# Folding two adapted linear layers on one core: the first product by pairs of k over all columns, the bias sum dealt out in single steps, the folded adapters stored in three chunks, and sixteen turns of the identity as TensorE's first work

## The reference

```python
x = x + L0_ffn(L0_cond(x, lang_ids))
x = x + L1_ffn(L1_cond(x, slot_ids))
```

```python
# L0_cond: x @ W.T + 2 * top-2 gated LoRA (8 experts of rank 16, a bias of 5.0 for the batch's language)
# L0_ffn : top-1 gated LoRA alone, no base product
# L1_cond: x @ W.T + b + 2 * (x @ lora_As[slot]) @ lora_Bs[slot]   (one adapter per batch, 32 slots)
# L1_ffn : y @ W_base.T + b_base + 2 * top-2 gated LoRA
```

## Time and profile before

| | |
|---|---|
| time, median of 3 runs | 466.93 us (466.07 to 467.23) |
| the profiled execution: its own time | 465.49 us |
| its span, first to last instruction | 463.6 us |
| PE busy | 446.5 us (96%) |
| DVE, ACT, POOL busy | 307.6, 154.8, 68.6 us |
| moved by DMA | 37.08 MB |

### The profile page before, as it was taken

One profiled execution on the slowest core, in us unless ns is written; L12 is line 12 of the kernel. 1 busy time (PEld: TensorE's weight loads), 2 busy tenths in 40 slices (PEclk: granted clock), 3 DMA queues, 4 the chain that ended last, 5 costly groups with the idle time before them and its releaser, 6 DMA issues.

```text
span 463.6 us, 7831 instructions
## 1 busy us (share of the span) xinstructions
PE 446.5 (96%) x2758; PEld 414.8 (89%) x2758; DVE 307.6 (66%) x916; ACT 154.8 (33%) x325; POOL 68.6 (15%) x61
## 2 busy tenths in 40 slices
PE   4999989999969999999999999999999999999997
PEld 4988989999968898889899999999999999999986
DVE  4856675656996788578467648738747755864852
ACT  5754363202122463234233224224323423321310
POOL 1100000000002411402402222120140230220110
PEclk9999999999998999999999999999999999999999
DMA  8973651101110101104102201211210310300202
GB/s 270 386 216 134 207 216 45 47 0 47 53 39 6 50 23 49 47 17 145 47 11 104 79 17 62 98 46 62 98 45 17 139 54 1 111 7 1 107 2 90
DMA packets 16287, 37.08 MB, mean 80 GB/s; under 512 B 2551, under 2 KB 7929, under 8 KB 16254
## 3 DMA queue, kind: packets, MB, share of 16 engines
q1 hardware_dynamic: 16158, 36.66, 23.1%
q0 software_dynamic: 96, 0.00, 0.0%
HBM read 27.07 MB, written 9.59 MB: 79 GB/s over the span
## 4 chain that ended last, share of the span: by engine, by line
PE 72%; DVE 14%; SPq 6%; DMA 3%; issue 2%; ACT 2%; DVEq 0%; ACTq 0%
PE banks L1334 22%; PE banks L1336 22%; PE banks L1335 22%; SPq L330 5%; DVE b_acc L1097 3%; DVE G L852 3%; PE banks L1422 2%; PE banks L1567 2%; DMA ws_lo_raw<-in_W_dram 2%; DMA b0lo_raw<-in_W_dram 1%; DVE ws_lo L852 1%; PE banks L1349 1%; SPq L362 1%; DVE x_raw L998 1%; DVE left L852 1%
## 5 line engine op out<-in xcount | busy, mean ns | idle before, releaser
L1334 PE MATMUL banks<-G,left 128*128 128x460 f32 x224 | 88.0, 393 | 0.0
L1335 PE MATMUL banks<-G,left 128*128 128x460 f32 x224 | 82.9, 370 | 0.0
L1336 PE MATMUL banks<-G,left 128*128 128x460 f32 x224 | 82.9, 370 | 0.0
L1334 PE MATMUL banks<-WbThi,ws_hi 128*128 128x460 f32 (+1 forms) x192 | 68.4, 356 | 9.8 <-DVE WbTlo L852 5.5
L509 POOL TENSOR_TENSOR xTlo<-x_raw,xThi 128x512 fp32r<-128x512 f32 x28 | 37.9, 1373 | 209.7 <-DVE hg L910 107.4
L1336 PE MATMUL banks<-WbThi,ws_lo 128*128 128x460 f32 (+1 forms) x192 | 67.0, 349 | 0.0
L1335 PE MATMUL banks<-WbTlo,ws_hi 128*128 128x460 f32 (+1 forms) x192 | 66.9, 348 | 0.0
L561 ACT ACTIVATE left<-x_raw 128x512 fp32r<-128x512 f32 x64 | 38.7, 627 | 59.9 <-DVE x_raw L998 29.3
L1334 PEld LDWEIGHTS banks<-WbThi,ws_hi 128*128 128x128 f32 x192 | 38.0, 198 | 13.1 <-issue 6.2
L1334 PEld LDWEIGHTS banks<-G,left 128*128 128x128 f32 x224 | 42.5, 190 | 4.5 <-DVE wzTlo L852 0.3
L1336 PEld LDWEIGHTS banks<-G,left 128*128 128x128 f32 x224 | 42.0, 188 | 4.7
(11 more groups left out here) (208 smaller groups left out, 964.1 us busy)
## 6 DMA issues: line engine op xcount, KB each, us to landing
x_raw<-in_xT_dram SPq DMA_DIRECT2D x16, 512.0 KB, 3.7
out_dram<-ybuf SPq DMA_DIRECT2D x14, 512.0 KB, 2.7
WbTlo_raw<-in_F_dram SPq DMA_DIRECT2D x8, 460.0 KB, 8.3
x_raw<-in_W_dram SPq DMA_DIRECT2D x6, 512.0 KB, 3.7
ws_lo_raw<-in_W_dram SPq DMA_DIRECT2D x3, 512.0 KB, 5.1
w0s_lo_raw<-in_W_dram SPq DMA_DIRECT2D x2, 512.0 KB, 9.5
Fbuf<-fe_hi_dram SPq DMA_DIRECT2D x16, 64.0 KB
ws_lo_raw<-in_W_dram SPq DMA_DIRECT2D x3, 256.0 KB, 5.0
```

The lines of the kernel that those rows point to most:

```text
L1334: pe.matmul(out_, l[0], r[0], start=start, stop=False, **kw)
L1335: pe.matmul(out_, l[0], r[1], start=False, stop=False, **kw)
L1336: return pe.matmul(out_, l[1], r[0], start=False, stop=stop, **kw)
```

## The change

1. **By pairs of k over all columns.** The first two block rows are no longer made chunk by chunk. For k 0 and 1, rows 0 and 1 get c0, then c1, then c2; then the same for k 2 and 3, and so on (`first_two`). `WF_PARTS` (now six pieces) and `F_PARTS` (still 11, another order) and the lists of SP, ACT and DVE follow. The 144 matmuls are the same.
2. **Sixteen turns of the identity**, on a PSUM place that nothing reads, as TensorE's first instructions, after POOL has built the identity.
3. **`ids` early**: POOL loads the ids before it waits for the splits. SP's place for reading them stays.
4. **The adapters' split moved up**: the ACT and DVE halves of `bs` (lines 561 and 852) now stand ahead of `fold_rows(0)`; before, they stood behind it.
5. **The folded adapters stored by chunk**: six stores, two for each chunk, in place of two. The first four stand ahead of the load of W0's block 3, the last two behind it.
6. **`b_acc` dealt out**: `b_times(first, last)` counts halves. Halves stand as 1, 3, 1, 3, 3 and 5 between other steps, all ahead of `fold_rows(5)`; before, they stood by whole k as 2, 2, 2, 6 and, behind `fold_rows(5)`, 4.
7. On ACT, in the loop over rows 2 to 5, `w1_split` no longer waits for `m_ident`, only for the row's last matmul.

```diff
-        WF_PARTS = [(0, 0, 2), (0, 2, 4), (1, 0, 4), (0, 4, 8), (1, 4, 8)]
+        WF_PARTS = [(0, 0, 2), (1, 0, 2), (0, 2, 4), (1, 2, 4), (0, 4, K), (1, 4, K)]
...
-        F_PARTS = [(0, 0, 2), (0, 2, 4), (0, 4, K), *((c, k, k + 2) for c in (1, 2) for k in range(0, K, 2))]
+        F_PARTS = [(0, 0, 2), (1, 0, 2), (2, 0, 2), (0, 2, 4), (1, 2, 4), (2, 2, 4),
+                   (0, 4, K), (1, 4, 6), (2, 4, 6), (1, 6, K), (2, 6, K)]
...
             load_wf(0)
             load_f(0)
+            load_wf(1)
             load_f(1)
-            load_wf(1)
+            load_f(2)
             load_wf(2)
+            load_f(3)
             load_wf(3)
-            load_f(2)
+            load_f(4)
+            load_f(5)
             load_wf(4)
-            for i in range(3, 11):
+            load_f(6)
+            load_wf(5)
+            for i in range(7, 11):
                 load_f(i)
...
+            def store_fe(c):
+                s = slice(CHUNKS[c][0], CHUNKS[c][0] + CHUNKS[c][1])
+                sp.wait_ge(fe_hi, c + 1)
+                sp.wait_ge(fe_lo, c + 1)
+                sp.dma_start(fe_hi_dram[0:P, s], fe_keep[0][:, s].bitcast(F32)).then_inc(fe_stored, 16)
+                sp.dma_start(fe_lo_dram[0:P, s], fe_keep[1][:, s].bitcast(F32)).then_inc(fe_stored, 16)
+
+            store_fe(0)
+            store_fe(1)
             sp.wait_ge(fe_done, 3)
             load_w0(3)
-            sp.wait_ge(fe_hi, 3)
-            sp.wait_ge(fe_lo, 3)
-            sp.dma_start(fe_hi_dram[0:P, :], fe_keep[0][:, :].bitcast(F32)).then_inc(fe_stored, 16)
-            sp.dma_start(fe_lo_dram[0:P, :], fe_keep[1][:, :].bitcast(F32)).then_inc(fe_stored, 16)
+            store_fe(2)
             sp.wait_ge(d0w_done, 1)
             load_w0(4)
...
-            gp.wait_ge(wf_hi, 5)
             gp.dma_start(ids[0:1, 0:NB], lang_ids.rearrange("(a b) -> a b", a=1)).then_inc(ids_in, 16)
             gp.dma_start(ids[0:1, NB:2 * NB], slot_ids.rearrange("(a b) -> a b", a=1)).then_inc(ids_in, 16)
+            gp.wait_ge(wf_hi, 6)
...
             hi_half(a0_in, 16, a0_part(C0hi), a0_part(C0raw), a0_hi)
+            hi_half(bs_in, 16 * NB, k_first(bs_hi_t), by_batch(bs_raw), bs_hi)
             act.wait_ge(m_ident, 1)
...
-            hi_half(bs_in, 16 * NB, k_first(bs_hi_t), by_batch(bs_raw), bs_hi)
...
-                act.wait_ge(m_ident, s + 1)
                 act.wait_ge(m_done, m_count(s, 2))
                 w1_split(s + 2)
+                act.wait_ge(m_ident, s + 1)
...
             lo_in(a0_hi, 1, a0_part(C0lo), a0_part(C0raw), a0_part(C0hi), a0_lo)
+            lo_in(bs_hi, 1, k_first(bs_lo_t), by_batch(bs_raw), k_first(bs_hi_t), bs_lo)
             dve.wait_ge(ident_ready, 1)
             fold_rows(0)
-            lo_in(bs_hi, 1, k_first(bs_lo_t), by_batch(bs_raw), k_first(bs_hi_t), bs_lo)
...
             gates0(0, 0)
-            hgT_part(0)
             dve.wait_ge(bcol_in, 16)
             dve.wait_ge(bbase_in, 16)
-            b_times(0)
+            b_times(0, 1)
+            hgT_part(0)
+            b_times(1, 4)
             top1(0)
             fold_rows(2)
             whT_part(0, 0)
             gates0(1, 0)
+            b_times(4, 5)
             hgT_part(1)
-            b_times(1)
+            b_times(5, 8)
             top1(1)
             fold_rows(3)
             whT_part(1, 1)
+            b_times(8, 11)
             for g in range(2):
                 x1_add(0, g, x_raw0, X1W_FIRST[g])
-            b_times(2)
             fold_rows(4)
             for g in range(2, 4):
                 x1_add(0, g, x_raw0, X1W_FIRST[g])
-            for k in range(3, 6):
-                b_times(k)
+            b_times(11, 2 * K)
             fold_rows(5)
-            for k in range(6, K):
-                b_times(k)
...
+            def first_two(c, k0, k1, split):
                 for par in range(2):
-                    m_steps(par, 1, k, k + 2)
-            for k in range(0, K, 2):
-                pe.wait_ge(f_lo, 8 + k // 2)
-                m_steps(0, 2, k, k + 2)
-            m_chunk(1, 2)
+                    pe.wait_ge(f_lo, split)
+                    if c == 0:
+                        pe.wait_ge(wf_lo, min(2 * (k0 // 2), 4) + par + 1)
+                    m_steps(par, c, k0, k1)
+
+            pe.wait_ge(ident_ready, 1)
+            for _ in range(16):
+                pe.transpose(pt_h1, ident[:, :], ident[:, :])
+            first_two(0, 0, 2, 1)
+            first_two(1, 0, 2, 2)
+            first_two(2, 0, 2, 3)
+            first_two(0, 2, 4, 4)
...
```

More of the change, by code:

```diff
@@ L159, in adaln_ffn @@
         w0_in, w0_hi, w0_lo = [sem(f"w0_in{i}") for i in range(K)], sem("w0_hi"), sem("w0_lo")
[L160 removed]
+        wf_in, wf_hi, wf_lo = [sem(f"wf_in{i}") for i in range(6)], sem("wf_hi"), sem("wf_lo")
         b0_in, b0_hi, b0_lo = sem("b0_in"), sem("b0_hi"), sem("b0_lo")
@@ L1088, in keep_fe, with b_times @@
                 lo(fe_keep[1][:, c0:c0 + n], m_psum(0, c), fe_keep[0][:, c0:c0 + n], 2.0).then_inc(fe_lo, 1)
-            def b_times(k):
-                for n in range(2):
+            def b_times(first, last):
+                for nth in range(first, last):
+                    k, n = nth // 2, nth % 2
                     for c, (c0, w) in enumerate(CHUNKS):
-                        nth = 2 * k + n
                         dve.wait_ge(acc_step, 3 * nth + c - 1 if nth else 1)
```

54 lines of the change are left out of this document (28 added, 26 removed).

## The result

| | before | changed |
|---|---|---|
| median, us | 466.42 (465.74 to 467.23, 6 runs) | 461.07 (460.61 to 462.87, 6 runs) |
| profiled execution, us | 465.49, span 463.6 | 460.61, span 458.8 |

The ratio is 0.9892, 95% interval 0.9872 to 0.9912: the changed kernel is 1.1% faster, against a forecast of 462.0. By medians the late part wins more and the start loses more, about 6.5 and 1 us; a good part of that is half clock that the one profile of the kernel before doesn't show (see "The late part alone").

What follows compares the result with a forecast made beforehand. TensorE was taken as the bound, busy 446.5 of 463.6 us, leaving only waits and half-clock matmuls to win. Terms -3.6 -1.6 +0.3 = -4.9 from 465.49 gave 460.6; the median, 1.44 higher, was forecast at 462.0, range 460.1 to 464.9.

Steps and rivals of the forecast that it cites:

- `ids` early: At the start, POOL's earlier id load: costed at nothing, since SP's own list covers it; without that list, more.
- The sum: Whole kernel: -3.6 -1.6 +0.3 = -4.9 us against the profiled 465.49, so 460.6; median forecast 462.0.
- The base: Starting time: the profiled execution's 465.49 us, with the median of the runs standing 1.44 us above it.
- The bias and ACT's order: Late folding, at fold_rows(5): TensorE's 3.8 us wait for Mdir shrinks to 0.3, worth -3.6 us from start to start.
- The half clock behind it: Behind the late Mdir wait: the 3.4 us slow stretch returns to full clock, -1.6 us, ends 0 and -1.7.
- The M stage: First two rows by pairs of k: matmuls end near 33 us, between 30.5 and 34.7; the gain ends waiting for adapters.
- rival C: New gaps before FE and at blocks 3 and 4 bring half clock back: 464.7 us, chance 0.14.
- The stores by chunk: Around 50 to 61 us: block 3 issued at 51.9, a new wait of 1 us there, block 4 starting at 61.3.
- +0.3: At block 4 of W0: TensorE starts at 61.3 in place of 61.0 us; ends -0.5 and +1.4.
- B: At block 4: chunk 0's early store unloads the queue, so it lands a microsecond or more earlier; 460.3 us, chance 0.11.
- D: At fold_rows(5) or an earlier step: DVE is late and the bias only moves the wait; 466.8 us, chance 0.07.
- E: At block 4: six stores cost like three times two, delaying it +8.5 us; 470.2 us, chance 0.05.

Runs made afterwards that it cites:

- undo_both: The changed kernel with the bias by whole k as before and ACT's W1 split again behind the identity: 467.77 us, ratio 1.0028.
- undo_act: The changed kernel with only ACT's split of W1 put back behind the wait for the identity: 462.70 us, ratio 0.9912.
- keep_early: The changed kernel with DVE taking chunk 1's low half straight behind chunk 0's, ahead of a W0 split and the language bias: 459.77 us, ratio 0.9874.
- store_mid: The changed kernel with chunk 1's pair of stores moved behind block 3's load: 459.95 us, ratio 0.9875.
- adapters_first: The changed kernel with the eight lora_Bs loads issued ahead of R0, W0(0), B0 and A0, and split first: 459.56 us, ratio 0.9845.
- undo_stores: The changed kernel with two whole stores behind block 3's load, as before the change: 460.18 us, ratio 0.9888.
- undo_bias: The changed kernel with only the bias dealt by whole k as before: 463.48 us, ratio 0.9916.
- bias_only: The kernel before with only the bias dealt out and ACT's W1 split moved ahead of the identity: 460.08 us, ratio 0.9852.

## Why the prediction was right, point by point

- **The sum.** -4.9 us against the profiled execution was forecast, 465.49 to 460.61 measured. The median came out at 461.07 and not 462.0, because I set it 1.44 us above the profiled execution; with all six runs that distance was 0.9 before and 0.5 after. The base was the step that was taken too lightly: one profile, of an execution with less half clock than most. By medians the late part wins 6.3 to 6.6 us and not 5.2, and the start loses about 1.0 and not 0.3. These two errors cancel, and that the median came so near is in part luck.
- **The bias and ACT's order.** Confirmed step by step. The late halves were to end at 129.7 and ended at 129.2; `fold_rows(5)` at 130.3, measured 130.56; row 7 at 133.1, measured 133.35; the wait 0.3, measured 0.3 (the two matmuls above start 0.40 us apart, against 0.11 without a wait). By `undo_both` this is worth 3.6 us up to row 7, as forecast. The step "ACT's split starts at 130.3" counted ACT's order as one step among others; the runs show it could carry most of the gain alone, as could the dealing. The forecast also left out what that order gives DVE earlier. Its waits of 1.1 us for ACT's split at `fold_rows(2)` to `fold_rows(4)` are gone too, so the three halves ahead of the sums of x, which were to overrun by 0.8 us, ended with 0.44 to spare, and the late halves half a microsecond earlier than forecast.
- **The half clock behind it.** Gone, and back in `undo_both`. The forecast was -1.6. From row 7 on the profiles give 326.9 before (463.6 - 136.68) and 325.4 after, so -1.5. `undo_both` gives 328.3: with the longer half clock the same edits save 2.8 us there, for which the stated end of -1.7 had no room.
- **The M stage.** Mis-sized: I expected an end near 33, and it ended where it had, at 34.7. The step "can't be out of operands so long" left out that behind a gap of 2 us half clock came back (rival C's mechanism, which I had put only before FE and at blocks 3 and 4). Where it did not, as in `undo_both`, `undo_act` and `keep_early`, the last matmul of the stage starts at 32.9 to 33.6, which is the 33. It cost nothing here, since the adapters gate FE, as I had said: FE at 35.56 (35.3 to 35.4), with 0.9 us of wait in place of 2.5. In `store_mid`, with 6.8 us of half clock, the stage itself gated FE, at 36.67.
- **`ids` early.** Nothing, confirmed in the trace: SP reads the first id at 18.00, behind its load of A0. The remark that without SP's own list it could have won more was worth a run: the median of `adapters_first` is 1.5 us under the changed kernel's.
- **The stores by chunk.** Block 3 was to be issued at 51.9 (measured 51.52), the wait to be 1 us (1.1) and block 4 to start at 61.3 (61.30): the last two came out to the tenth in that execution. But it was the earliest of its kind: the six profiles with this order of stores and the adapters' split as in the change start block 4 at 61.3 to 63.2, and the medians put the new start's cost at about 1 us. So over many executions "+0.3" is the term that was too small, inside its ends of -0.5 and +1.4, and its exact hit in this one is luck.
- **The rivals.** B would have needed chunk 1's pair elsewhere. In `store_mid` block 4 does start 1.2 us earlier, but no earlier than in `undo_stores`, which has no early store, so B's reason isn't what did it. C's mechanism came in the changed kernel in the first 12 us, where it cost nothing, but not at its gaps of 1.1 and 0.8 us at blocks 3 and 4. It did come at block 3 in `undo_bias`, behind 1.79 us of idle, and there block 4 started 3.5 us behind block 3, against 3.0 in `undo_act`: half a microsecond. D did not come. Nor did E: a pair held SP for 0.85 us (50.67 to 51.52), and block 4 had landed when ACT began to split it at 58.94.

What stays open: executions of the same start differ by up to 2 us at block 4. The changed kernel, `undo_both`, `undo_bias` and `undo_act` are the same program up to there and begin it at 61.30, 62.38, 63.20 and 63.11. The DMA rate from 4 to 36 us is 304 GB/s in the profile of `undo_act` (block 4 at 63.11), 326 in that of `keep_early` (59.10) and 337 in that of `adapters_first` (59.13), which fits a start bound by its loads, but no run held the rate fixed. So the small differences between `keep_early`, `store_mid`, `undo_stores` and `bias_only` are not told apart.

## What to carry to other kernels

Look for a landmark behind which all variants take the same time; then a change of many parts splits into what comes before it and what comes after, and a profile of each variant prices both, as long as what lies behind the landmark has the same granted clock in each. A single profile isn't enough for a base: look at the clock of the other runs too. When two edits relieve the same wait, undo both and each: here each alone kept 70% of the gain or more. And before a transfer is put in a queue ahead of a load that is needed, look at what it waits for on the engine that makes its data: the small stores were cheap, but SyncE stood for a low half that VectorE made 2.5 us later than it could.
